# Attention on one core: the row of maxima for the queries, from four products with the identity and a copy to two transfers through memory

## The chip, the cores and the metric

The kernel runs on one core of a Trainium2 chip. Its engines are TensorE (PE in the profile, its weight loads PEld), VectorE (DVE), ScalarE (ACT), GpSimd (POOL) and SyncE (SP), which here issues transfers; 16 DMA engines move the data. Each engine works through its own list of instructions in order and waits on semaphores for the others. The metric is the device time of one execution in microseconds; lower is better.

## The reference, cut to what matters

Two layers, each `x = x + attention(norm(x)) * silu(ffn(norm(x)))`, on 2048 tokens of width 128. Attention has 16 heads of width 64:

```python
# layer 0                                             # layer 1, with rotated q, k
scores = einsum('bhsd,bhtd->bhst', q, k) * scale      scores = einsum('bhqd,bhkd->bhqk', q, k) * SCALE
                                                      kb = -p * jnp.log1p(a * dist)
attn = softmax(scores, axis=-1)                       attn = softmax(scores + kb[None], axis=-1)
out = einsum('bhst,bhtd->bhsd', attn, v)              out = einsum('bhqk,bhkd->bhqd', attn, v)
out = einsum('bsf,fm->bsm', out, WO[0])               out = out @ out_w.T
```

Scores are large, so the softmax needs each query's maximum subtracted before the exponential. In this kernel the scores stand transposed, keys on partitions and queries along the free dimension; the maxima must therefore lie in a row along the queries.

## The kernel before

`attention_stage` runs once for each layer. The work of a layer is cut into 64 chunks (`NCH`): 16 heads (`H`) by 4 groups of 512 queries (`NC`, `QC`). A chunk `n` has 8 steps (`NS`), each with 256 keys. The order of each engine is written out by hand.

What happens to the maxima, by the lines of the profile:

- TensorE, `maxima(n, j)` (L652, L653): 128 queries by 1024 keys, into the PSUM buffer `jb` (in the first two chunks also into the two halves of `st`). VectorE reduces each product to one maximum for each query (`maxima`: L845 in layer 0; in layer 1 L840, which adds the bias table on the way) and signals `max_done`; only then may TensorE write `jb` again. This runs two chunks ahead (`AHEAD`).
- VectorE, `merge(n)` (L851): eight partial maxima for each partition become `m4`, four numbers on each of 128 partitions.
- ScalarE, `divide_maxima(n)` (L772): `m4` divided by 128 is written as fp16 into `m4w`, spread over 128 columns in layer 0 and over two columns (0 and 64, of an otherwise zero tile) in layer 1.
- TensorE, `row(n)` (L663): four products of `m4w` with the identity put the numbers along the free dimension of `xb`, a PSUM buffer that the sums (`sums_of`, L710) and the projection (`project`, L719) use too.
- ScalarE, `row(n)` (L777): `xb` is copied to `rows[:, n % 2, :]`, fp16, and signals `row_done`.
- Use: `scores(n, s)` on TensorE (L688) accumulates q times k in three rounds of two products and, in a fourth, `lower` times `rows`, which subtracts the maxima. In layer 0 only every other step has the fourth round; in the others VectorE subtracts (`subtract_maxima`, L865), reading `rows` from SBUF. In layer 1 all steps have it, and VectorE adds the bias table (`add_bias`, L878). Then ScalarE takes the exponential (L784, L788, L795), GpSimd adds up the sums (L943 to L950), and TensorE multiplies by the values (`values`, L699).

The row of chunk `n + 1` is made inside chunk `n`: at step 5 in layer 0 and at step 1 in layer 1 (`ROW_STEP`); the sums of the chunk before stand at step 3, its projection at step 7 or 5. TensorE takes the steps of layer 0 in pairs: a maxima product, scores of two steps, a second maxima product, whatever `between` puts there, values of two steps. Such a pair is called a slot below. Ahead of the loop TensorE makes all maxima products of chunk 0, the row of chunk 0, and the maxima products of chunk 1.

SP's queue holds the loads of the queries and keys of a head, high and low halves (`qh`, `kh`, `ql`, `kl`, eight transfers of 256 KB), and in layer 1 the bias table (`tab`). The loads of head `h` wait until the loads of the head before have landed and the scores of head `h - 2` have been read.

Of the kernel before, what the change touches and what calls it, by code (L numbers as in the profile page):

```python
# [11 lines left out]
P = 128  # L12
D = 128
S = 2048
# [23 lines left out]
SUM_STEP, ROW_STEP, OUT_STEP = (3, 3), (5, 1), (7, 5)  # L38
# [526 lines left out]
def attention_stage(nc, k, layer, bias=False):  # L565

    with ExitStack() as ctx:
# [6 lines left out]
        m4w = m.sb(g + "m4w", [P, 4, P], F16)  # L574
# [16 lines left out]
        row_ready, row_done = m.sem(g + "row_ready"), m.sem(g + "row_done")  # L591
# [7 lines left out]
        sum_step, row_step, out_step = SUM_STEP[layer], ROW_STEP[layer], OUT_STEP[layer]  # L599
# [19 lines left out]
        def _(sp):  # L619
            for h in range(H):  # L620
                if h >= 1:
                    sp.wait_ge(loaded, 16 * loads * h)
                    sp.wait_ge(low_loaded, 16 * 4 * h)
                if h >= 2:
                    sp.wait_ge(st_read, NS * NC * (h - 1))
# [7 lines left out]
                if h == 0:  # L633
                    sp.wait_ge(loaded, 16 * loads)
                for low in (slice(0, DH), slice(DH, P)):
                    sp.dma_start(ql[low, at], k.qk_low[0, pr][half, :]).then_inc(low_loaded, 16)
                    sp.dma_start(kl[low, at], k.qk_low[1, pr][half, :]).then_inc(low_loaded, 16)

        @block.tensor
        def _(pe):  # L640
# [15 lines left out]
            def row(n):  # L656
                pe.wait_ge(m4_done, n + 1)
                if bias and n >= 3:
                    pe.wait_ge(proj_done, n - 2)
                if not bias and n >= 2:  # L660
                    pe.wait_ge(rs_done, n - 1)
                for t in range(4):
                    last = nc.tensor.matmul(xb[:, t * P:(t + 1) * P], m4w[:, t, :], k.ident16[:, :],  # L663
                                            start=True, stop=True)
                last.then_inc(row_ready, 1)

            def scores(n, s):
# [3 lines left out]
                if s == 0:  # L671
                    pe.wait_ge(row_done, n + 1)
# [31 lines left out]
            def sums_of(n):  # L704
                pe.wait_ge(folded, n + 1)
                pe.wait_ge(row_done, min(n + (3 if bias else 2), NCH))
# [7 lines left out]
            def project(n):  # L714
                pe.wait_ge(ov_saved, n + 1)
                pe.wait_ge(rs_done, n + 1)
                pe.wait_ge(row_done, min(n + 3, NCH))
# [8 lines left out]
            row(0)  # L726
# [6 lines left out]
            def between(n, s):  # L733
                if s == row_step and n + 1 < NCH:
                    row(n + 1)
# [643 lines left out]
```

## Time and profile before

| | |
|---|---|
| time, median of 3 runs | 3077.13 us (3074.41 to 3077.42) |
| the profiled execution | 3079.59 us |
| its span, first to last instruction | 3077.9 us |
| TensorE busy | 2807.8 us, 91% |
| VectorE busy | 2504.0 us, 81% |
| GpSimd busy | 2502.6 us, 81% |
| ScalarE busy | 1557.4 us, 51% |
| packets of all transfers | 63825, of these 18017 under 512 B |

Times in the rows are microseconds from the start of the span. Attention of layer 0 lies between about 194 and 1435, that of layer 1 between about 1731 and 3067; what stands before, between and behind is norms, feed-forward parts and the making of q, k and v. A row of a timeline gives start, length, engine, line, operation and operands; the bracket at its end, where there is one, is the time the engine sat idle before it and what it waited for. Products that follow one another are pipelined, so their lengths overlap.

### The profile page before, as it was taken

To read this page: it belongs to the slowest core of one execution; us is meant where nothing else is said; L and a number is where in the kernel's file an instruction comes from. 1 tells how busy PE (TensorE), PEld (TensorE's weight loads), DVE (VectorE), ACT (ScalarE), POOL (GpSimd) and SP (SyncE) were. 2 spreads that over 40 slices of the span, in tenths; PEclk is the share of its full clock that TensorE was granted. 3 is DMA by queue.
4 is the path that set the end of the run, shared out by engine and by line. 5 is a ranking of instruction groups with operands and counts; after the bars stand their busy time and mean duration, and the time that the engine had idled before them with its cause. 6 is when DMAs were issued, how large, how long until landed. Compare 5 with 4: busy or idle time off the path is not lost. (4 is left out here: it accounts for less than half of the span.)

```text
span 3077.9 us, 46733 instructions
## 1 busy us (share of the span) xinstructions
PE 2807.8 (91%) x17656; PEld 1147.6 (37%) x17656; DVE 2504.0 (81%) x3379; ACT 1557.4 (51%) x1889; POOL 2502.6 (81%) x1205
## 2 busy tenths in 40 slices
PE   5959999999999999996499599999999999999997
PEld 3413333333333333333354133333333333333332
DVE  6568888888888888874339699999999999999995
ACT  4325555555555555552122255555555555555554
POOL 0009999999999999994339389999999999999997
PEclk9979999999999999997699699999999999999998
DMA  4250111111111111101203501111111111111100
GB/s 109 86 191 22 35 29 28 28 28 28 28 28 28 28 29 28 28 1 38 60 27 137 190 4 52 55 55 55 55 55 55 55 55 55 55 55 55 55 1 14
DMA packets 63825, 155.28 MB, mean 50 GB/s; under 512 B 18017, under 2 KB 33770, under 8 KB 61426
## 3 DMA queue, kind: packets, MB, share of 16 engines
q1 hardware_dynamic: 62578, 150.20, 17.4%
q8 instruction: 141, 2.31, 0.3%
q0 software_dynamic: 1024, 2.10, 0.2%
q14 instruction: 82, 0.67, 0.1%
HBM read 113.34 MB, written 38.93 MB: 49 GB/s over the span
## 5 line engine op out<-in xcount | busy, mean ns | idle before, releaser
L943 POOL TENSOR_TENSOR a_sums<-a_sums,room 128x1024 f32<-128x1024 f32 x512 | 1195.4, 2364 | 83.1 <-ACT room L795 42.5
L699 PE MATMUL a_ov<-room,va 128*64 128x512 f32 x4096 | 994.0, 606 | 0.0
L784 ACT ACTIVATE room<-room,sscale 128x1024 f32<-128x1024 f32 x512 | 588.3, 1149 | 539.3 <-DVE room L878 539.2
L845 DVE TENSOR_REDUCE a_mx<-a_jb 128x1 f32<-128x1024 f32 x501 | 611.9, 1221 | 129.6 <-PE a_jb L653 123.4
L943 POOL TENSOR_TENSOR a_sums<-room 128x1024 f32<-128x1024 f32 x256 | 604.3, 2361 | 116.6 <-ACT room L784 66.8
L840 DVE CUSTOM_DVE_ANT_0 a_junk<-a_jb,a_tab 128x1024 bf16<-128x1024 f32 x501 | 610.5, 1219 | 83.2 <-PE a_jb L653 74.8
L878 DVE TENSOR_TENSOR room<-a_st,a_tab 128x1024 f32<-128x1024 f32 x512 | 622.9, 1217 | 12.4 <-PE a_st L688 10.2
L795 ACT ACTIVATE room<-a_st,sscale 128x1024 f32<-128x1024 f32 x256 | 285.3, 1114 | 360.1 <-PE a_st L688 360.1
L652 PE MATMUL a_jb<-a_kh,a_qh 64*128 64x512 f16 x1002 | 384.9, 384 | 66.1 <-DVE a_mx L840 32.1
L699 PEld LDWEIGHTS a_ov<-room,va 128*64 128x64 f32 x4096 | 248.7, 136 | 409.3 <-issue 372.7
L688 PE MATMUL a_st<-a_qh,a_kh 64*128 64x512 f16 x2048 | 395.6, 383 | 3.0 <-DVE a_mx L840 2.9
L688 PE MATMUL a_st<-a_ql,a_kh 64*128 64x512 f16 x2048 | 390.8, 378 | 0.0
L688 PE MATMUL a_st<-a_qh,a_kl 64*128 64x512 f16 x2048 | 390.6, 378 | 0.0
L865 DVE SCALAR_TENSOR_TENSOR room<-a_rows,a_st 128x1024 f32<-128x1024 f16 x256 | 312.7, 1221 | 92.3 <-PE a_st L688 90.9
L653 PE MATMUL a_jb<-a_kh,a_qh 64*128 64x512 f16 x1002 | 385.1, 384 | 0.0
L788 ACT ACTIVATE room<-room,sscale 128x1024 f32<-128x1024 f32 x256 | 294.0, 1148 | 170.8 <-DVE room L865 170.8
L946 POOL TENSOR_TENSOR a_sums<-a_sums 128x1024 f32<-128x1024 f32 x128 | 302.8, 2366 | 10.1
L688 PE MATMUL a_st<-a_rows,a_lower 64*128 64x512 f16 x1536 | 292.9, 378 | 0.0
L652 PEld LDWEIGHTS a_jb<-a_kh,a_qh 64*128 64x128 f16 x1002 | 93.6, 93 | 465.8 <-DVE a_mx L845 306.3
L688 PEld LDWEIGHTS a_st<-a_qh,a_kh 64*128 64x128 f16 x2048 | 99.8, 94 | 274.0 <-issue 164.1
L950 POOL TENSOR_TENSOR a_total<-a_sums 128x512 f32<-128x512 f32 x128 | 162.5, 1270 | 10.0
L710 PE MATMUL a_xb<-ones,a_total 128*128 128x1 f32 x1024 | 136.4, 254 | 17.3 <-POOL a_total L950 17.3
(219 smaller groups left out, 2642.6 us busy)
## 6 DMA issues: line engine op xcount, KB each, us to landing
a_tab<-bias_line SPq DMA_DIRECT2D x16, 1984.0 KB, 11.0
qk_high<-q_oh SPq DMA_DIRECT2D x32, 512.0 KB, 2.6
qk_low<-q_ol SPq DMA_DIRECT2D x32, 512.0 KB, 3.6
a_qh<-qk_high SPq DMA_DIRECT2D x64, 256.0 KB, 4.5
a_kh<-qk_high SPq DMA_DIRECT2D x64, 256.0 KB, 5.1
a_ql<-qk_low SPq DMA_DIRECT2D x64, 256.0 KB, 7.5
a_kl<-qk_low SPq DMA_DIRECT2D x64, 256.0 KB, 7.8
ex_w<-in_L_ffn_W SPq DMA_DIRECT2D x1, 2048.0 KB, 10.5
```

The costliest lines, as they stand in the source:

```text
L652: nc.tensor.matmul(o[:, 0:QC], qh[0:DH, q0:q0 + P], kh[0:DH, k0:k0 + QC], start=True, stop=True)
L653: nc.tensor.matmul(o[:, QC:2 * QC], qh[DH:P, q0:q0 + P], kh[DH:P, k0 + QC:k0 + 2 * QC], start=True, stop=True).then_inc(max_ready, 1)
L688: last = nc.tensor.matmul(st[:, step % 2, t * QC:(t + 1) * QC], w, x, start=(r == 0), stop=(r == len(rounds) - 1))
L699: last = nc.tensor.matmul(ov[t * DH:(t + 1) * DH, :], k.va[:, 2 * s + t, h * DH:(h + 1) * DH], prob[:, step % RING, t * QC:(t + 1) * QC], ...
L784: nc.scalar.activation(prob[:, r, :], prob[:, r, :], ACT.Exp, scale=k.sscale[:, layer:layer + 1])\
L788: nc.scalar.activation(prob[:, r, :], prob[:, r, :], ACT.Exp, scale=k.sscale[:, 0:1])\
L840: nc.vector.tensor_tensor_reduce(out=junk[:, i % 2, :], in0=scratch(n, j), in1=tab[:, n // NC % 2, c0:c0 + 2 * QC][:, ::-1], scale=1.0, sc ...
L845: nc.vector.reduce_max(mx[:, j // 2, j % 2:j % 2 + 1], scratch(n, j), AX.X).then_inc(max_done, 1)
L865: nc.vector.scalar_tensor_tensor(p, high, -float(MAXROW), x, ALU.mult, ALU.add).then_inc(lowered, 1)
L878: nc.vector.tensor_tensor(p[:, :, ::-1], x[:, :, ::-1], window, ALU.add).then_inc(added, 1)
L943: nc.gpsimd.tensor_tensor(a, first, prob[:, step % RING, :], ALU.add).then_inc(summed, 1)
L946: nc.gpsimd.tensor_tensor(a, a, sums[:, (n + 1) % 2, :], ALU.add).then_inc(summed, 1)
```

## The change

`m4` divided by 128 becomes `m4h`, 128 partitions by 4 numbers in fp16. SP stores it into a row of memory, `max_row[layer, n]`, as 512 single elements in the order of the queries, waits for the store, and loads that row into all 128 partitions of `rows[:, n % 2, :]` with one transfer. TensorE's `row(n)`, ScalarE's `row(n)`, the tile `m4w` and its memset go, and with them the waits that kept `xb` apart from the row. Those who waited for `row_done` wait for `row_in`. The loads of a head stand in SP's queue behind a row's broadcast.

```diff
-        m4w = m.sb(g + "m4w", [P, 4, P], F16)
+        m4h = m.sb(g + "m4h", [P, 4], F16)
...
+            def spread_row(n):
+                sp.wait_ge(m4_done, n + 1)
+                sp.dma_start(k.max_row[layer, n].rearrange("(t p) -> p t", p=P), m4h[:, :],
+                             allow_slow_non_contiguous=True).then_inc(row_stored, 16)
+                sp.wait_ge(row_stored, 16 * (n + 1))
+                if n >= 2:
+                    sp.wait_ge(st_ready, NS * (n - 1))
+                    if not bias:
+                        sp.wait_ge(lowered, NS // 2 * (n - 1))
+                sp.dma_start(rows[:, n % 2, :], k.max_row[layer, n:n + 1, :].broadcast_to([P, QC])).then_inc(row_in, 16)
+
+            high_and_bias(0)
+            sp.wait_ge(loaded, 16 * loads)
+            low_halves(0)
+            spread_row(0)
+            sp.wait_ge(low_loaded, 16 * 4)
+            high_and_bias(1)
+            low_halves(1)
+            for n in range(NCH - 1):
+                sp.wait_ge(row_in, 16 * (n + 1))
+                spread_row(n + 1)
+                h = n // NC + 1
+                if n % NC == 0 and 2 <= h < H:
+                    sp.wait_ge(loaded, 16 * loads * h)
+                    sp.wait_ge(low_loaded, 16 * 4 * h)
+                    sp.wait_ge(st_read, NS * NC * (h - 1))
+                    high_and_bias(h)
+                    low_halves(h)
...
-            def row(n):
-                pe.wait_ge(m4_done, n + 1)
-                if bias and n >= 3:
-                    pe.wait_ge(proj_done, n - 2)
-                if not bias and n >= 2:
-                    pe.wait_ge(rs_done, n - 1)
-                for t in range(4):
-                    last = nc.tensor.matmul(xb[:, t * P:(t + 1) * P], m4w[:, t, :], k.ident16[:, :],
-                                            start=True, stop=True)
-                last.then_inc(row_ready, 1)
-
...
                 if s == 0:
-                    pe.wait_ge(row_done, n + 1)
+                    pe.wait_ge(row_in, 16 * (n + 1))
...
                 if n >= 1:
-                    act.wait_ge(row_ready, n)
-                wide = m4w[:, :, 0:DH + 1:DH] if bias else m4w[:, :, :]
-                nc.scalar.activation(wide, m4[:, :].unsqueeze(2).broadcast_to([P, 4, 2 if bias else P]), ACT.Copy,
-                                     scale=1.0 / MAXROW).then_inc(m4_done, 1)
-
-            def row(n):
-                act.wait_ge(row_ready, n + 1)
-                nc.scalar.activation(rows[:, n % 2, :], xb[:, :], ACT.Copy).then_inc(row_done, 1)
+                    act.wait_ge(row_stored, 16 * n)
+                nc.scalar.activation(m4h[:, :], m4[:, :], ACT.Copy, scale=1.0 / MAXROW).then_inc(m4_done, 1)
```

TensorE inside the loop of layer 0, the end of the slot with the row, before:

```order
L652 MATMUL a_jb<-a_kh,a_qh 128x512 [waits a0_max_done]
L653 MATMUL a_jb<-a_kh,a_qh 128x512
L663 MATMUL a_xb<-ident,a_m4w 128x128 [waits a0_rs_done,a0_m4_done]
L663 MATMUL a_xb<-ident,a_m4w 128x128 x3
L699 MATMUL a_ov<-room,va 64x512 [waits a0_exp_done]
```

The same place in the changed kernel, where a slot with the row now reads like the empty one:

```order
L678 MATMUL a_jb<-a_kh,a_qh 128x512 [waits a0_max_done]
L679 MATMUL a_jb<-a_kh,a_qh 128x512
L714 MATMUL a_ov<-room,va 64x512 [waits a0_exp_done]
L714 MATMUL a_ov<-room,va 64x512
L714 MATMUL a_ov<-room,va 64x512 [waits a0_exp_done]
```

The row's four products, and their wait for the divided maxima, are gone between the maxima product and the values.

TensorE ahead of the loop of layer 0, from the last two maxima products of chunk 0 to the first of chunk 1, before:

```order
L652 MATMUL a_st<-a_kh,a_qh 128x512 [waits a0_max_done]
L653 MATMUL a_st<-a_kh,a_qh 128x512
L663 MATMUL a_xb<-ident,a_m4w 128x128 [waits a0_m4_done]
L663 MATMUL a_xb<-ident,a_m4w 128x128 x3
L652 MATMUL a_jb<-a_kh,a_qh 128x512 [waits a0_max_done]
L653 MATMUL a_jb<-a_kh,a_qh 128x512
```

And in the changed kernel:

```order
L678 MATMUL a_st<-a_kh,a_qh 128x512 [waits a0_max_done]
L679 MATMUL a_st<-a_kh,a_qh 128x512
L678 MATMUL a_jb<-a_kh,a_qh 128x512 [waits a0_max_done]
L679 MATMUL a_jb<-a_kh,a_qh 128x512
L678 MATMUL a_st<-a_kh,a_qh 128x512 [waits a0_max_done]
```

The wait for the divided maxima of chunk 0 no longer stands ahead of chunk 1's first maxima product.

SP in layer 0 of the changed kernel, around the loads of head 2 (`a0_m4_done` is ScalarE's signal that `m4h` is written, `a0_row_in` that a broadcast landed):

```order
L638 DMA max_row<-a_m4h 128x4x1 [waits a0_m4_done,a0_row_in]
L645 DMA a_rows<-max_row 128x512 [waits a0_lowered,a0_st_ready,a0_row_stored]
L624 DMA a_qh<-qk_high 64x2048 [waits a0_exp_done,a0_low_loaded,a0_loaded]
L625 DMA a_kh<-qk_high 64x2048
L624 DMA a_qh<-qk_high 64x2048
L625 DMA a_kh<-qk_high 64x2048
L633 DMA a_ql<-qk_low 64x2048
L634 DMA a_kl<-qk_low 64x2048
L633 DMA a_ql<-qk_low 64x2048
L634 DMA a_kl<-qk_low 64x2048
L638 DMA max_row<-a_m4h 128x4x1 [waits a0_m4_done,a0_row_in]
```

In the kernel before, that queue held the eight loads alone, head behind head; now each row's store and broadcast stand among them.

## Rows read from the trace of the kernel before

**Rows 1.** Stretches inside layers 0 and 1: us, busy by engine, clock, DMA, GB/s

```profile
630.00:930.00 300.00, 294.21 (x2004) 117.23 (x2002) 249.63 (x291) 169.91 (x179) 283.75 (x130) 1.00 0.13 29
2300.00:2600.00 300.00, 291.35 (x1961) 110.09 (x1963) 279.30 (x388) 169.74 (x225) 281.55 (x134) 1.00 0.20 56
```

The busy columns are TensorE, its weight loads, VectorE, ScalarE and GpSimd.

**Rows 2.** Timeline of TensorE in layer 0: row's slot, projection's end, empty slot

```profile
607.13 0.39 PE L652 MATMUL a_jb<-a_kh,a_qh 64*128 64x512 f16 x1
...
609.18 0.40 PE L663 MATMUL a_xb<-ident,a_m4w 128*128 128x128 f16 x4
609.51 1.94 PE L699 MATMUL a_ov<-room,va 128*64 128x512 f32 x8
611.49 0.39 PE L652 MATMUL a_jb<-a_kh,a_qh 64*128 64x512 f16 x1
...
614.63 1.94 PE L699 MATMUL a_ov<-room,va 128*64 128x512 f32 x8
616.50 0.39 PE L652 MATMUL a_jb<-a_kh,a_qh 64*128 64x512 f16 x1
...
620.85 0.39 PE L652 MATMUL a_jb<-a_kh,a_qh 64*128 64x512 f16 x1 [0.32 <-DVE a_mx L845]
```

**Rows 3.** Timeline of VectorE in the slot with the row, layer 0

```profile
609.08 1.22 DVE L865 SCALAR_TENSOR_TENSOR room<-a_rows,a_st 128x1024 f32<-128x1024 f16 x1 [0.29 <-PE a_st L688]
...
610.22 1.22 DVE L845 TENSOR_REDUCE a_mx<-a_jb 128x1 f32<-128x1024 f32 x1
```

**Rows 4.** Timeline of all engines around the row in layer 1

```profile
2213.49 0.40 PE L663 MATMUL a_xb<-ident,a_m4w 128*128 128x128 f16 x4
2213.62 1.22 DVE L840 CUSTOM_DVE_ANT_0 a_junk<-a_jb,a_tab 128x1024 bf16<-128x1024 f32 x1
...
2213.82 0.39 PE L688 MATMUL a_st<-a_qh,a_kh 64*128 64x512 f16 x2
...
2214.89 0.09 PEld L652 LDWEIGHTS a_jb<-a_kh,a_qh 64*128 64x128 f16 x1 [0.53 <-DVE a_mx L840]
```

**Rows 5.** Timeline ahead of the loops: layer 0, then layer 1

```profile
211.07 0.63 ACT L772 ACTIVATE a_m4w<-a_m 128x512 f16<-128x512 f32 x1 [23.77 <-DVE a_m L851]
...
213.01 1.22 DVE L845 TENSOR_REDUCE a_mx<-a_jb 128x1 f32<-128x1024 f32 x1 [2.04 <-PE a_jb L653]
...
222.61 0.63 PE L688 MATMUL a_st<-a_qh,a_kh 64*128 64x512 f16 x2
...
1753.08 0.24 ACT L772 ACTIVATE a_m4w<-a_m 128x8 f16<-128x8 f32 x1 [22.75 <-DVE a_m L851]
...
1754.66 1.23 DVE L840 CUSTOM_DVE_ANT_0 a_junk<-a_jb,a_tab 128x1024 bf16<-128x1024 f32 x1 [1.67 <-PE a_jb L653]
...
1764.05 0.61 PE L688 MATMUL a_st<-a_qh,a_kh 64*128 64x512 f16 x2 [2.91 <-DVE a_mx L840]
```

**Rows 6.** Timeline: maxima divided in layers 0 and 1; first scores of layer 1's next chunk

```profile
604.54 0.62 ACT L772 ACTIVATE a_m4w<-a_m 128x512 f16<-128x512 f32 x1
...
2212.99 0.23 ACT L772 ACTIVATE a_m4w<-a_m 128x8 f16<-128x8 f32 x1
...
2227.63 0.39 PE L688 MATMUL a_st<-a_qh,a_kh 64*128 64x512 f16 x2
```

**Rows 7.** Transfers alike: an issue and who waited; issues, KB, us to landing

```profile
27.16 0.43 SPq L183 DMA_DIRECT2D tf_b<-in_L_ffn_b  x1
...
30.41 1.15 ACT L211 ACTIVATE tf_mag<-tf_w 128x512 f32<-128x512 f32 x2 [4.48 <-DMA tf_b<-in_L_ffn_b]
...
bias_line<-line SPq DMA_DIRECT2D x1, 256.0 KB, 2.0
...
rt_gain<-in_L_ffn_ln_g SPq DMA_DIRECT2D x1, 64.0 KB, 2.9
```

**Rows 8.** A head's last load in layer 1: its issue, then us to landing

```profile
2253.32 0.68 SPq L637 DMA_DIRECT2D a_kl<-qk_low  x1
...
a_kl<-qk_low SPq DMA_DIRECT2D x2, 256.0 KB, 11.9
```

More of the change, by code:

```diff
@@ L37 @@
 NJ = 8
-SUM_STEP, ROW_STEP, OUT_STEP = (3, 3), (5, 1), (7, 5)
+SUM_STEP, OUT_STEP = (3, 3), (7, 5)
 class Memory:
@@ L590, in attention_stage @@
         merged, m4_done = m.sem(g + "merged"), m.sem(g + "m4_done")
[L591 removed]
+        row_stored, row_in = m.sem(g + "row_stored"), m.sem(g + "row_in")
         st_ready, exp_done = m.sem(g + "st_ready"), m.sem(g + "exp_done")
@@ L598, in attention_stage @@
                                                                                    if bias else None)
-        sum_step, row_step, out_step = SUM_STEP[layer], ROW_STEP[layer], OUT_STEP[layer]
+        sum_step, out_step = SUM_STEP[layer], OUT_STEP[layer]
         lowered = None if bias else m.sem(g + "lowered")
@@ L619, in _, with high_and_bias @@
         def _(sp):
[L620 to L625, printed above, removed]
+            def high_and_bias(h):
                 at = slice((h % 2) * S, (h % 2 + 1) * S)
@@ L632, in _, with low_halves @@
                     sp.dma_start(tab[:, h % 2, :], k.bias_rows(h)).then_inc(loaded, 16)
-                if h == 0:
-                    sp.wait_ge(loaded, 16 * loads)
+            def low_halves(h):
+                at = slice((h % 2) * S, (h % 2 + 1) * S)
+                pr, half = h // 2, slice((h % 2) * DH, (h % 2 + 1) * DH)
                 for low in (slice(0, DH), slice(DH, P)):
@@ L725, in _ @@
                 maxima(0, j)
-            row(0)
             for j in range(NJ):
@@ L733, in between @@
             def between(n, s):
-                if s == row_step and n + 1 < NCH:
-                    row(n + 1)
                 if s == sum_step and n >= 1:
@@ L814, in _ @@
             divide_maxima(0)
-            row(0)
             for n in range(NCH):
@@ L822, in _ @@
                         divide_maxima(n + 1)
-                    if s == row_step and n + 1 < NCH:
-                        row(n + 1)
                     if bias and s == out_step and n >= 1:
@@ L857, in subtract_maxima @@
                 if s == 1:
-                    ve.wait_ge(row_done, n + 1)
+                    ve.wait_ge(row_in, 16 * (n + 1))
                 if step >= RING:
@@ L919, in _ @@
         def _(pool):
-            pieces = (flat(m4w[:, :, :]), lower[:, :], flat(k.acc[:, :, :]))
+            pieces = (lower[:, :], flat(k.acc[:, :, :]))
             for piece in pieces:
@@ L1328, in build @@
         k.qk_low = nc.dram_tensor("qk_low", (2, H // 2, P, S), F16, kind="Internal").ap()
+        k.max_row = nc.dram_tensor("max_row", (2, NCH, QC), F16, kind="Internal").ap()
         k.bias_line = nc.dram_tensor("bias_line", (H, LINE), F32, kind="Internal").ap()
```

2 lines of the change are left out of this document (removed).

## The prediction

> **What bounds the kernel now.** I read the stretches of the two attention stages first. In both, TensorE is busy 97 to 98% of the time at a granted clock of 1.00, GpSimd about 94%, VectorE 83 and 93%, ScalarE 57% [rows 1]. That invites a quick answer: take matmuls away from TensorE and the time falls by their length. A busy TensorE need not be the engine that ends a slot, though, so the second view is its timeline through one chunk of layer 0.
>
> A chunk of layer 0 has four slots. Each begins with a maxima product into `jb`, runs scores and a second maxima product, and ends with the products of probabilities and values. One slot also holds the sums, one the row, one the projection, and one nothing extra. The slot with the row goes from 607.13 to 611.49, which is 4.36 us; the empty slot from 616.50 to 620.85, 4.35 us [rows 2]. The row's four products move the next TensorE work by 609.51 - 609.18 = 0.33 us, and yet the slot is no longer than the one without them. What ends both slots stands on VectorE. The empty slot's end says so itself: its last row waits for `a_mx` on VectorE [rows 2]. In the row's slot VectorE waits 0.29 us for the scores, subtracts the maxima from 609.08, and reduces the second maxima product from 610.22 for 1.22 us, until 611.44 [rows 3]. TensorE begins the next maxima product at 611.49: `jb` is one buffer, and is free only then. By its own work TensorE would have been ready 1.87 us (the length of such a block where nothing holds it, 614.63 to 616.50) after 609.51, at 611.38 [rows 2]. So the row lies in 0.33 us that TensorE would otherwise have spent waiting.
>
> In layer 1 the row stands after the maxima product of step 1. It goes from 2213.49 to 2213.82, one block of scores follows, and the weights of the next maxima product are loaded at 2214.89, after a wait of 0.53 us that the row puts down to `a_mx` on VectorE. VectorE's reduction that frees `jb` runs from 2213.62 for 1.22 us, to 2214.84 [rows 4], 0.05 us before. So here too VectorE sets the slot's end.
>
> **The change part by part.** *Products removed.* Layer by layer 64 rows of 0.33 us go, 128 x 0.33 = 42 us of TensorE's work. In the steady loop (63 rows in each layer) I count nothing for them: cover is the chain scores, subtraction, reduction in layer 0 and back-to-back VectorE work in layer 1, neither of which reads `xb`. In layer 0 the removal makes at best 4.36 into 4.35 us, 63 x 0.01 = 0.6 us. If that cover were absent, they would be worth the whole 42 us.
>
> *ScalarE.* The widened copy of 0.62 us becomes one of 128x4, about 0.23 us by the 128x8 form [rows 6], and a 128x512 copy from PSUM (about 0.6 us) goes. ScalarE is busy 57% [rows 1] and neither copy stands before an exponent that is late, so this counts zero. What it does is to set the time at which the store may go.
>
> *The first rows.* Before the loop TensorE stops at the row of chunk 0 until the maxima are divided, and only then begins the maxima products of chunk 1, so VectorE sits idle: 2.04 us in layer 0 and 1.67 us in layer 1 [rows 5]. With the row gone TensorE goes on, its three buffers are free in turn, and VectorE passes from the merge to chunk 1 at once. The stages' first scores wait for VectorE's sixteenth reduction. That takes 2.04 + 1.67 = 3.7 us off, provided the row itself is there in time.
>
> *The two transfers.* From the division of the maxima to the first scores that read the row there are these spans. In layer 0's loop from 604.54 + 0.23 = 604.8 [rows 6] to 616.50 [rows 2], 11.7 us. In layer 1's loop from 2212.99 + 0.23 = 2213.2 to 2227.63, 14.4 us [rows 6]. In the first chunk of layer 0 from 211.07 + 0.23 = 211.3 to 222.61 - 2.04 = 220.6, 9.3 us; of layer 1 from 1753.32 to 1764.05 - 1.67 = 1762.4, 9.1 us [rows 5]. The trace has no store of 2-byte pieces, so I bound it by neighbours. From below: a store of whole rows to memory lands 2.0 us after its issue [rows 7]. From above: the load of `tf_b` has the same 512 single elements, 4 bytes each; it is issued at 27.16 behind that stage's weights, and the work that waits for all of them starts at 30.41, so it had landed within 3.2 us [rows 7]. I take 3.2, the row nearest in shape. The broadcast of one row to 128 partitions is like that of `rt_gain`, 2.9 us, with other loads ahead of it [rows 7]; from below it can hardly beat the 2.0 us of the store. Together 4.0 to 6.1 us, and with 6.1 still 3.0 us before the earliest deadline. So they are hidden in all four places, and count zero. With the cover gone each microsecond over costs 63 us in layer 0.
>
> That load shows 512 separate pieces costing little. It writes SBUF, however, and the new store writes memory, where no row has pieces so small. The Trainium skill (DMA: Bandwidth & Descriptors, Specifications) says that an engine carries out transfers below 512 B as read-modify-write; no run here shows it, and the page has no price for it. By the row the term is zero; by the page it would be the slow store below.
>
> *SP's queue.* Each row adds two issues there, and waits for the divided maxima, the store and the broadcast. Behind them queue the loads of the next head, which in the loop now leave after the row's broadcast is issued instead of at the chunk's start. In layer 1 these are nine issues of some 0.6 us, and the last such transfer lands 11.9 us after its issue [rows 8], some 17 us after the first issue. Now they begin about 4 us after the division (3.2 for the store, 0.6 for an issue), land some 21 us after it, and their first reader comes two chunks (40 us) later. The next row's store comes one chunk, 20 us, after the last; at worst it queues for 1 us behind their tail, against 14.4 - 6.1 = 8.3 us to spare. In layer 0, where only half as much is loaded, they are gone by then. Cost zero.
>
> **Sum.** The profiled execution took 3079.59 us, its span is 3077.9. 3079.59 - 3.7 - 0.6 = 3075.3. That execution lies 2.5 us over the median of the runs, 3077.13, so the forecast is 3072.8 us, 0.14% less. A measurement of this kernel tells some 0.2% (6.2 us) from no change, so this counts as the same.
>
> **The rivals.** *TensorE is the bound after all*: removed work comes back in full, 3077.1 - 42 - 4 = 3031 us. For it speak 98% [rows 1]; against it the two equal slots [rows 2]. A part of it is likelier, such as 0.1 to 0.3 us in one layer, 6 to 20 us: 3053 to 3067. It would need VectorE's chain to shorten too, and nothing in the change shortens it.
>
> *A slow store, the slower side.* Each of the 16 DMA engines has 32 pieces. Should they go one at a time to memory, the deadline in layer 0 falls when the store takes over 11.7 - 2.9 = 8.8 us, that is (8.8 - 2.0) / 32 = 0.21 us a piece. At 0.25 us the store takes 10.0 us, each of 63 chunks is 1.2 us longer: 3072.8 + 76 = 3149, with another 2.9 us in each first chunk, some 3155 us. Layer 1's 14.4 us would still hold. Against it speaks the load of the same number of pieces within 3.2 us.
>
> *The prologue's gain is lost.* If store and broadcast take 11 us, some 2 us more than the first chunks give them, they still fit into 11.7 and 14.4 us in the loop, but VectorE's 2.04 and 1.67 us turn into TensorE's wait for the row: 3076.5, no change. I count this with the main case.
>
> *Loads and rows in each other's way* at the 28 head changes that the loops have: if the next row waited so long behind the loads that its span were overrun by 0.2 to 0.6 us each time, 3078 to 3090. It decides from 8.3 us behind the tail in layer 1, and by the sum above 1 us is the most.
>
> **How the numbers follow.** Hidden transfers with all or some of the first chunks' gain 0.74 (3069.5 to 3079 with the runs' spread of 3 us; 0.05 of it falls below 3071, which is faster by over 0.2%). TensorE's time back in full 0.04, in part 0.07. Slow store 0.07. Loads and rows colliding 0.05, half of it over 3083. Something unnamed that is slower 0.03. So faster 0.16, slower 0.12 (0.07 + 0.02 + 0.03), same 0.72. For the range 0.8 is wanted: the main case, the better half of the partial gain and the collisions give 0.74 + 0.03 + 0.05, so from 3062 to 3086.
>
> **What would show it.** In the trace after: no products with `m4w`; a slot of layer 0 without sums and projection still 4.35 us, VectorE's reduction ending 0.05 us before TensorE's maxima product; VectorE's idle time ahead of chunk 1 near zero in both layers; the store landing in 2 to 3.2 us and the broadcast in 2 to 2.9; no wait of TensorE for `a_rows`; 64 x 512 more packets under 512 B in each layer. A row slot shorter than 4.3 us would prove the first rival; scores that wait for the broadcast in every chunk of layer 0 the second.

## The result: 4076.85 us, a third slower

| | before | after |
|---|---|---|
| time, median | 3075.78 us (3074.41 to 3077.42, 4 runs) | 4076.85 us (4058.95 to 4079.02, 4 runs) |
| ratio to before, 95% interval | | 1.3242 (1.3203 to 1.328) |
| profiled execution; its span | 3079.59; 3077.9 us | 4076.74; 4075.0 us |
| mean clock granted to TensorE over the span (1.00 is 2.4 GHz) | 0.964 | 0.867 |

The forecast was 3072.8 us, the range 3062 to 3086. It was wrong: the kernel is 1001 us slower. Three lines of the changed kernel's page: busy time by engine, the costliest group of scores on TensorE (busy, mean ns | idle time ahead of it and what ended it), and the broadcasts.

```profile
PE 3021.1 (74%) x17144; PEld 1176.7 (29%) x17144; DVE 2508.2 (62%) x3379; ACT 1472.6 (36%) x1761; POOL 2501.2 (61%) x1203
...
L703 PE MATMUL a_st<-a_qh,a_kh 64*128 64x512 f16 x2048 | 450.8, 437 | 802.7 <-DMA a_rows<-max_row 796.6
...
a_rows<-max_row SPq DMA_DIRECT2D x128, 128.0 KB, 4.5
```

TensorE has 512 instructions fewer than before, the row's products, and yet is busy longer: 3021.1 us instead of 2807.8. It is idle for 796.6 us ahead of scores that wait for the row's broadcast. The same two stretches as in [rows 1] (us; busy by TensorE, weight loads, VectorE, ScalarE, GpSimd; clock, DMA, GB/s):

```profile
630.00:930.00 300.00, 220.86 (x1326) 82.68 (x1328) 170.59 (x198) 106.66 (x110) 196.90 (x90) 0.88 0.18 27
2600.00:2900.00 300.00, 232.68 (x1411) 84.22 (x1410) 207.91 (x287) 119.94 (x154) 208.49 (x100) 0.88 0.21 47
```

Where 2004 matmuls ran in 300 us of layer 0, 1326 do now, and the granted clock is 0.88 instead of 1.00. SP's timeline in layer 0, the issues of one store, its broadcast and the next store:

```profile
721.54 0.37 SPq L638 DMA_DIRECT2D max_row<-a_m4h  x1
734.97 0.32 SPq L645 DMA_DIRECT2D a_rows<-max_row  x1
748.52 0.37 SPq L638 DMA_DIRECT2D max_row<-a_m4h  x1
```

SP issues the broadcast as soon as the store has landed, so the store takes 13.4 us. The prediction had 3.2. The next row, 27.0 us later, shows the new period. TensorE and VectorE where that broadcast lands, with two earlier rows of TensorE that bound a slot of the same chunk which has neither sums nor projection, the row's former slot:

```profile
723.86 0.39 PE L678 MATMUL a_jb<-a_kh,a_qh 64*128 64x512 f16 x1
728.22 0.39 PE L678 MATMUL a_jb<-a_kh,a_qh 64*128 64x512 f16 x1 [0.37 <-DVE a_mx L846]
...
739.42 0.61 PE L703 MATMUL a_st<-a_qh,a_kh 64*128 64x512 f16 x2 [5.81 <-DMA a_rows<-max_row]
...
742.63 1.22 DVE L866 SCALAR_TENSOR_TENSOR room<-a_rows,a_st 128x1024 f32<-128x1024 f16 x1 [7.68 <-PE a_st L703]
```

From 734.97 to 739.42 the broadcast takes 4.4 us (2.9 predicted). TensorE has waited 5.81 us for it, and its next products take 0.61 us instead of 0.39, the 1.2 GHz level. The slot without extra work, 723.86 to 728.22, is 4.36 us long and ends in a wait for VectorE, as in [rows 2].

So each chunk is now one closed chain: maxima divided, store, broadcast, first scores, and some steps later the next chunk's maxima divided. The starts of the 128 divisions in ScalarE's timeline give the periods; the first of each layer is left out of the means. In layer 0 they go from 18.61 to 27.00 us in the mean, 63 x 8.39 = 529 us. In layer 1 they go from 20.20 to 27.54, 63 x 7.34 = 462 us. Together that is 991 of the 997 us by which the spans of the two profiled executions differ.

When do the pieces move? Two stretches behind the store at 721.54 (columns as above):

```profile
722.50:723.00 0.50, 0.50 (x6) 0.21 (x4) 0.50 (x1) 0.50 (x1) 0.00 (x0) 1.00 0.49 18
723.00:734.50 11.50, 10.24 (x68) 3.67 (x64) 9.39 (x14) 4.84 (x5) 10.50 (x5) 1.00 0.01 1
```

The DMA engines are half busy for half a microsecond, then almost idle (a share of 0.01) for 11.5 us, until the store counts as landed. The store's time is not in packets that engines handle one behind the other; it lies after them. The Trainium skill (DMA: Bandwidth & Descriptors, Anatomy of one DMA) says, of transfers that GpSimd issues, that the semaphore can only be raised once the last byte is confirmed in the target memory, and puts most of a fixed 2 us there. This transfer is SP's; its trace agrees on the place, not on the size: from 723.04, when the last 2-byte packet has moved, to 734.97 are 11.9 us.

### The profile page after: what moved, and what is told of

It is laid out like the page before. It is cut to its first block and busy times, and to the rows that moved or that the text cites. A ratio compares the mean times of both kernels' runs of the same rounds, so it can differ in the third digit from the quotient of the medians.

```text
span 4075.0 us, 45958 instructions
## 1 busy us (share of the span) xinstructions
PE 3021.1 (74%) x17144; PEld 1176.7 (29%) x17144; DVE 2508.2 (62%) x3379; ACT 1472.6 (36%) x1761; POOL 2501.2 (61%) x1203
## 5 line engine op out<-in xcount | busy, mean ns | idle before, releaser
L703 PE MATMUL a_st<-a_qh,a_kh 64*128 64x512 f16 x2048 | 450.8, 437 | 802.7 <-DMA a_rows<-max_row 796.6
L714 PE MATMUL a_ov<-room,va 128*64 128x512 f32 x4096 | 1040.4, 630 | 0.0
L879 DVE TENSOR_TENSOR room<-a_st,a_tab 128x1024 f32<-128x1024 f32 x512 | 622.9, 1217 | 30.4 <-PE a_st L703 28.2
L678 PE MATMUL a_jb<-a_kh,a_qh 64*128 64x512 f16 x1002 | 421.5, 421 | 62.1 <-DVE a_mx L846 34.0
L703 PE MATMUL a_st<-a_ql,a_kh 64*128 64x512 f16 x2048 | 450.7, 437 | 0.0
L703 PE MATMUL a_st<-a_qh,a_kl 64*128 64x512 f16 x2048 | 448.5, 434 | 0.0
L679 PE MATMUL a_jb<-a_kh,a_qh 64*128 64x512 f16 x1002 | 421.5, 421 | 0.0
L714 PEld LDWEIGHTS a_ov<-room,va 128*64 128x64 f32 x4096 | 262.0, 144 | 499.9 <-issue 419.7
L703 PE MATMUL a_st<-a_rows,a_lower 64*128 64x512 f16 x1536 | 334.7, 432 | 0.0
L703 PEld LDWEIGHTS a_st<-a_qh,a_kl 64*128 64x128 f16 x2048 | 112.8, 107 | 159.0 <-issue 66.4
## 6 DMA issues: line engine op xcount, KB each, us to landing
a_tab<-bias_line SPq DMA_DIRECT2D x16, 1984.0 KB, 14.4
```

The source lines that it names most:

```text
L678: nc.tensor.matmul(o[:, 0:QC], qh[0:DH, q0:q0 + P], kh[0:DH, k0:k0 + QC], start=True, stop=True)
L679: nc.tensor.matmul(o[:, QC:2 * QC], qh[DH:P, q0:q0 + P], kh[DH:P, k0 + QC:k0 + 2 * QC], start=True, stop=True).then_inc(max_ready, 1)
L703: last = nc.tensor.matmul(st[:, step % 2, t * QC:(t + 1) * QC], w, x, start=(r == 0), stop=(r == len(rounds) - 1))
L714: last = nc.tensor.matmul(ov[t * DH:(t + 1) * DH, :], k.va[:, 2 * s + t, h * DH:(h + 1) * DH], prob[:, step % RING, t * QC:(t + 1) * QC], ...
L879: nc.vector.tensor_tensor(p[:, :, ::-1], x[:, :, ::-1], window, ALU.add).then_inc(added, 1)
```

## Experiments: what the store waits for

**Trial transfers.** The kernel before, with single transfers from SP put behind the head loads of layer 0, each waited for; the code is cut to two of ten kinds:

```diff
+            def store_2(i):        # 512 x 2 B, adjacent
+                sp.dma_start(k.t_2[i].rearrange("(t p) -> p t", p=P), k.ident16[:, 0:4], ...).then_inc(probed, 16)
+            def store_2_at_64(i):  # 512 x 2 B, 64 B apart
+                sp.dma_start(k.t_2_64[i, :, 0].rearrange("(t p) -> p t", p=P), k.ident16[:, 0:4], ...).then_inc(probed, 16)
...
+                        probes[i % len(probes)](i // len(probes))
+                        sp.wait_ge(probed, 16 * (i + 1))
```

> The kernel before, with its row as it was, and beside it trial transfers on SP's otherwise idle queue in layer 0, four of each kind, one at a time, each waited for; nothing else waits for them, so the time stays near 3077. What is read is the time from a trial's issue to the next issue. Kinds: store of 512 pieces of 2 bytes next to one another (the change's own), load of the same, broadcast of a 1 KB row, store of 512 pieces of 4 bytes side by side, of 2 bytes each 64 bytes apart, of 2 bytes each 512 bytes apart, of 128 pieces of 8 bytes side by side, of 128 pieces of 2 bytes side by side, of 512 pieces of 64 bytes, of 512 pieces of 512 bytes. Theory A, each small write to memory costs its DMA engine a fixed time, (13.4 - 2.0) / 32 = 0.36 us: all kinds of 512 pieces under 512 bytes take 13 us, both kinds of 128 pieces 2.0 + 8 x 0.36 = 4.9 us. Theory B, writes into the same few bytes of memory stand in line: 13 us side by side, about 3 us at 64 or 512 bytes apart, 128 pieces some 5 us, 64-byte pieces 3 us. Theory C, 512 pieces are slow to issue or to count whichever way they go: the load takes 13 us too. By A and B the load stays under 3.2 us.

SP's timeline; from one issue to the next is the length of the first transfer, where a trial follows a trial (the last of a group of three is followed by the next head's loads and can't be read). `t` is the trial row of memory, L623 the adjacent 512 x 2 B, L641 the load of that row as 512 pieces, L629 and L632 512 x 2 B at 64 and at 512 B, L638 128 adjacent x 2 B, L626 512 adjacent x 4 B, L635 128 adjacent x 8 B:

```profile
217.94 0.38 SPq L623 DMA_DIRECT2D t<-ident  x1
232.03 0.38 SPq L641 DMA_DIRECT2D a_rows_back<-t  x1
235.56 0.33 SPq L650 DMA_DIRECT2D a_rows_back<-t  x1
...
386.55 0.34 SPq L638 DMA_DIRECT2D t<-ident  x1
402.29 0.37 SPq L644 DMA_DIRECT2D t<-gate  x1
...
539.01 0.37 SPq L626 DMA_DIRECT2D t<-gate  x1
548.08 0.36 SPq L629 DMA_DIRECT2D t<-ident  x1
...
612.35 0.34 SPq L635 DMA_DIRECT2D t<-ident  x1
615.03 0.33 SPq L638 DMA_DIRECT2D t<-ident  x1
...
834.30 0.36 SPq L629 DMA_DIRECT2D t<-ident  x1
836.07 0.37 SPq L632 DMA_DIRECT2D t<-ident  x1
838.03 0.33 SPq L635 DMA_DIRECT2D t<-ident  x1
```

| transfer | us, issue to next issue |
|---|---|
| store, 512 x 2 B adjacent | 12.9 to 14.1 |
| the same 512 pieces loaded into SBUF | 2.6 to 4.0 |
| that 1 KB row broadcast to 128 partitions | 2.9 |
| store, 512 x 2 B, 64 B apart; 512 B apart | 1.8 to 3.0; 1.8 to 2.0 |
| store, 512 x 4 B adjacent | 8.1 to 10.5 |
| store, 128 x 8 B adjacent | 2.7 to 3.9 |
| store, 128 x 2 B adjacent | 15.7 to 16.3 |
| store, 512 x 64 B; 512 x 512 B | 1.8 to 2.0; 2.3 |

Theory B holds in kind; it is not the count of pieces, and not their size: 512 pieces of 2 B are quick once they lie 64 B apart. The price is for small writes close together in memory; the load of the same pieces, which writes SBUF, is quick, which is why it was a bad neighbour to judge by. The surprise is that a quarter as many adjacent pieces take longer, 16 us against 13.

**How close together.** Other stores in the same place, all of 2-byte pieces from one column of a tile: 8, 32 and 64 adjacent ones, and 128 with gaps.

```diff
+            probes = (few(8), few(32), few(64), apart(2), apart(4), apart(8), apart(16))
```

> The kernel before with trial stores from SP in layer 0, each waited for, of 2-byte pieces out of one column of a tile. The changed kernel's store took 13.4 us; the first trial transfers gave some 13.3 us for 512 adjacent pieces of 2 bytes, 16 us for 128 adjacent ones, 2.2 us for 512 pieces that lie 64 B apart. Theory L (pieces that fall into the same 64 B of memory are written one behind the other, at 13.3 / 32 = some 0.4 us each, and different 64 B go side by side): 32 adjacent pieces (one such line) cost as much as 512, some 13 us, 64 adjacent ones too; 8 adjacent pieces some 3.3 us; 128 pieces 4 B apart (16 to a line) some 7 us, 8 B apart (8 to a line) some 3.5 us, 16 B apart (4 to a line) and 32 B apart (2 to a line) some 2 us. Theory T (the time goes with the number of adjacent pieces in the whole store, whatever line they are in): 8 pieces 2 us, 32 pieces some 4 us, 64 pieces some 8 us, half of 128's. Theory G (what counts is a gap, not the line: pieces with a gap between them are quick): all four with gaps 2 us.

SP's timeline, 8 adjacent pieces, then 32, and elsewhere 64 (`t_few`), each up to the next issue:

```profile
219.95 0.29 SPq L623 DMA_DIRECT2D t_few<-ident  x1
221.12 0.32 SPq L623 DMA_DIRECT2D t_few<-ident  x1
225.21 0.48 SPq L623 DMA_DIRECT2D t_few<-ident  x1
...
460.15 0.46 SPq L623 DMA_DIRECT2D t_few<-ident  x1
469.83 0.34 SPq L629 DMA_DIRECT2D t_apart<-ident  x1
```

8 pieces 1.2 us, 32 pieces 3.1 to 4.1, 64 pieces 9.7 to 11.9; 128 pieces 4 B apart 7.4 to 8.3, 8 B apart 3.0 to 5.1, 16 B apart 1.4 to 2.3, 32 B apart 1.4 to 1.5. The two longest stores of 64, 11.6 and 11.9 us, came right behind a trial store into the same row; the two of 9.7 us did not. Theory L, lines of 64 B, falls with the 32 pieces (13 us expected). Theory T, their mere number, falls with 512 pieces being no slower than 128. Theory G falls with the gaps of 2 B. Yet nearly all of it fits a coarser line: 0.1 to 0.16 us for each piece in the same 256 B (up to 0.19 in the two stores of 11.6 and 11.9 us), with different 256 B side by side. That rule was made from these numbers, so it needed a test of its own.

**Shifting the pieces.** The same stores, begun at other places of a 1 KB row:

```diff
+            probes = (at(0, 128), at(64, 128), at(0, 64), at(32, 64), at(96, 64), two_of_128, at(0, 32))
```

> The kernel before with trial stores of adjacent 2-byte pieces from SP in layer 0, shifted against the start of a 1 KB row of memory. All trial stores so far fit one rule: some 0.12 us for each piece that falls into the same 256 B, and different 256 B side by side (32 adjacent pieces 3.1 to 4.1 us, 64 9.7, 128 16, 512 13; 128 pieces 4 B apart 7.5, 8 B apart 3 to 5, 16 B apart 2.1, 32 B apart 1.4). Theory 256 (blocks of 256 B counted from the row's start): 128 pieces from byte 0 16 us, from byte 128 (64 in each of two blocks) some 9 us; 64 pieces from byte 0 and from byte 64 9.7 us, from byte 192 (32 and 32) some 4 us; 256 pieces in two blocks some 16 us; 32 from byte 0 some 3.5 us. Theory T (the number of adjacent pieces counts, wherever they begin): the shift changes nothing, and 256 pieces take longer than 128. Theory 512 (blocks of 512 B): no change with these shifts, and 256 pieces some 30 us.

SP's timeline: 128 pieces from byte 0, then 128 from byte 128; and from another head 64 pieces from byte 64, then 64 from byte 192:

```profile
218.73 0.33 SPq L623 DMA_DIRECT2D t_line<-ident  x1
234.29 0.33 SPq L623 DMA_DIRECT2D t_line<-ident  x1
244.53 0.47 SPq L623 DMA_DIRECT2D t_line<-ident  x1
...
836.92 0.46 SPq L623 DMA_DIRECT2D t_line<-ident  x1
843.42 0.46 SPq L623 DMA_DIRECT2D t_line<-ident  x1
847.51 0.38 SPq L628 DMA_DIRECT2D t_line<-ident  x1
```

| pieces, first byte | most in one 256 B | expected by it | measured, us |
|---|---|---|---|
| 128 from 0 | 128 | 16 | 15.6 to 16.8 |
| 128 from 128 | 64 | 9 | 8.5 to 10.2 |
| 64 from 0 | 64 | 9.7 | 8.7 to 9.7 |
| 64 from 64 | 64 | 9.7 | 6.5 to 8.1 |
| 64 from 192 | 32 | 4 | 3.3 to 4.3 |
| 256 from 0 | 128 | 16 | 15.0 to 16.8 |
| 32 from 0 | 32 | 3.5 | 3.0 to 4.4 |

Moving the same 128 pieces by 128 B makes their store a third to a half shorter, and a second block of 128 adds nothing. So it is the 256 B that count, by their place in the row, and not the number of pieces. Writes into one 256 B stretch of memory stand in line; the row of 64 from byte 64 is a little quicker than the rule has it. The kernel's 512 adjacent pieces are four such stretches of 128; they took 13 us where the rule says 16, and the trials don't show why. Of what in the memory or on the way to it makes them wait these runs say nothing.

## Experiments: what the change is worth with a quick store, and what its parts are worth

**The quick store.** The changed kernel, storing each partition's four maxima as one piece of 8 B (32 pieces in 256 B). The row then has another order, so the maxima of other queries are subtracted; the work is the same.

```diff
-                sp.dma_start(k.max_row[layer, n].rearrange("(t p) -> p t", p=P), m4h[:, :],
-                             allow_slow_non_contiguous=True).then_inc(row_stored, 16)
+                sp.dma_start(k.max_row[layer, n].rearrange("(p t) -> p t", p=P), m4h[:, :]).then_inc(row_stored, 16)
```

> The changed kernel with one line different: the store writes each partition's four numbers side by side, 128 pieces of 8 bytes in place of 512 of 2. The numbers of the row then stand in another order than the queries, so the softmax subtracts the maxima of other queries; everything else is as in the changed kernel. If the 2-byte pieces are the cause of the slow store, the store lands in 2 to 5 us, store and broadcast fit into the 9 to 14 us that the row has, and the time is what the prediction gave for hidden transfers, 3070 to 3077 us. If the way through memory is slow as such (two dependent transfers, the wait on SP, the broadcast), it stays over 3500 us.

3073.26 us (3071.53 to 3075.14), ratio 0.9993 (0.9984 to 1.0002). SP's timeline in layer 0, a store and its broadcast:

```profile
731.32 0.32 SPq L638 DMA_DIRECT2D max_row<-a_m4h  x1
733.96 0.32 SPq L644 DMA_DIRECT2D a_rows<-max_row  x1
```

And the broadcasts in the page's list of transfers, the last number being the median from issue to landing:

```profile
a_rows<-max_row SPq DMA_DIRECT2D x128, 128.0 KB, 4.1
```

With a store of 2.6 us here (2.9 in the median) the periods are 18.59 and 20.21 us, those of the kernel before, and the time is 0.5 us from the forecast. That near a hit has luck in it: the forecast took off 4.3 us, and against the kernel before, 3075.69 us in the same round, 2.4 came off (4.9 less to 0.6 more by the interval). All other terms of the sum held together; how the store lays its pieces makes the difference between 3073 and 4077 by itself.

**The order kept.** The same store, with each query getting its own maximum: in layer 0 a maxima product takes every fourth query, in layer 1 TensorE reads the row with a step of 8 B.

```diff
+        def in_order(n):
+            return rows[:, n % 2, :].rearrange("k (p t) -> k t p", t=4) if bias else rows[:, n % 2, :]
...
+                at = slice(q0 + j // 2 * P, q0 + (j // 2 + 1) * P) if bias else slice(q0 + j // 2, q0 + QC, 4)
-                nc.tensor.matmul(o[:, 0:QC], qh[0:DH, q0:q0 + P], kh[0:DH, k0:k0 + QC], start=True, stop=True)
+                nc.tensor.matmul(o[:, 0:QC], qh[0:DH, at], kh[0:DH, k0:k0 + QC], start=True, stop=True)
...
-                        x = rows[half, n % 2, :] if r == 3 else queries[half, q0:q0 + QC]
+                        x = in_order(n)[half] if r == 3 else queries[half, q0:q0 + QC]
```

> The changed kernel with the store as 128 pieces of 8 bytes, and everything else put so that each query still gets its own maximum: in layer 0 a maxima product takes every fourth query, so that a partition holds four neighbouring queries; in layer 1 TensorE reads the row in memory order with a step of 8 bytes. My theory (only the store's term was wrong, a store of 8-byte pieces takes 3 us and is hidden): 3073 us like the run in which the row's order was left wrong (3073.26), a ratio of 0.999 to the kernel before. Rival (reading or loading fp16 with a step of 8 bytes costs TensorE time): 8 weight loads of a chunk in layer 0 and 8 products of 64 x 512 in layer 1 (of 64) slower; if a product with such a step takes twice its time, 8 x 0.2 us in a chunk of layer 1, up to 100 us over: 3170 us.

3161.03 us, ratio 1.0279 (1.0265 to 1.0293): the rival holds. TensorE's timeline in layer 1, at a granted clock of 1.00 (window 2300 to 2600):

```profile
2300.68 0.38 PE L706 MATMUL a_st<-a_qh,a_kl 64*128 64x512 f16 x2
2300.90 0.61 PE L706 MATMUL a_st<-a_rows,a_lower 64*128 64x512 f16 x2
2301.33 0.40 PE L681 MATMUL a_jb<-a_kh,a_qh 64*128 64x512 f16 x1
```

The pair that reads the row with a step holds TensorE from 2300.90 to 2301.33, 0.43 us, where its neighbour takes 0.22. Eight such pairs are 1.7 us more a chunk; layer 1's period went from 20.20 to 21.54, layer 0's (18.67, with stepped weight loads) hardly moved. 63 x 1.34 = 84 us is the loss, but for 2 us. So the change can be made harmless in layer 0, but this way of putting the order right in layer 1 costs more than the row's products ever did.

**The row's products taken away.** The kernel before, making the row for chunks 0 and 1 alone; from chunk 2 on old rows are subtracted.

```diff
-                if s == row_step and n + 1 < NCH:
+                if s == row_step and n + 1 < 2:
                     row(n + 1)
```

> The kernel before without the row's four products and without the copy of the row in the loop, from chunk 2 on: scores read the rows of chunks 0 and 1 again and again, so other maxima are subtracted. If VectorE ends the slots with the row, as the prediction has it, the time falls by 0 to 1 us (3075 us). If TensorE is the bound, 124 x 0.33 = 41 us come off (3035 us).

3076.03 us, ratio 1.0003 (0.9994 to 1.0013). TensorE's busy time in the page fell from 2807.8 to 2765.0 us, and nothing came of it: the 42 us lay in TensorE's waits for VectorE, as the prediction said, and the rival in which TensorE is the bound is dead, its part of 6 to 20 us too: the interval leaves 2 us at most.

**The first row moved.** The kernel before, its first row made behind the third maxima product of chunk 1:

```diff
-            row(0)
             for j in range(NJ):
                 maxima(1, j)
+                if j == 2:
+                    row(0)
```

> The kernel before with one step moved: ahead of the loop the row of chunk 0 stands behind the third maxima product of chunk 1 and not ahead of the first. If VectorE's idle time there (2.04 and 1.67 us) sits on the path, the time falls by 3.7 us, to a ratio of 0.9988; if the first chunk is held by something else, it stays at 1.000.

3072.45 us, ratio 0.9986 (0.9977 to 0.9995), the one version whose interval lies wholly below the kernel before. VectorE's timeline ahead of layer 0's loop, where [rows 5] has 2.04 us of idle time:

```profile
207.93 0.16 DVE L852 TENSOR_REDUCE a_m<-a_mx 128x4 f32<-128x8 f32 x1
208.12 1.22 DVE L846 TENSOR_REDUCE a_mx<-a_jb 128x1 f32<-128x1024 f32 x1
```

The idle time is gone. The prediction's 3.7 us (0.12%) for the two stages lie inside the interval, which reaches from 0.05 to 0.23%.

## Experiments: from a late row to 1000 us

**Delay by other means.** The quick store made three and five times over, one waiting for the other:

```diff
+                for i in range(3):
+                    if i >= 1:
+                        sp.wait_ge(row_stored, 16 * (3 * n + i))
+                    sp.dma_start(k.max_row[layer, n].rearrange("(p t) -> p t", p=P), m4h[:, :]).then_inc(row_stored, 16)
```

> The changed kernel with the quick store of 128 pieces of 8 bytes (other queries' maxima are subtracted, as in the run with the quick store), made three times over, one waiting for the other, ahead of the broadcast: 3 x 2.9 + 4.1 = 12.8 us from the divided maxima to the row. The prediction's deadlines are 11.7 us in a chunk of layer 0, 14.4 in layer 1, 9.3 and 9.1 in the first chunks. If they hold and each microsecond over is one of time: layer 0 some 1.1 us over in 63 chunks, 69 us, and 3.5 us in each first chunk: 3073 + 76 = 3150 us, layer 1 unchanged. If the clock falls as soon as TensorE waits, more: 3200 us or over. If the deadlines are too tight (others wait with the row and have room), 3080 us or under.

> The same with five quick stores, one behind the other: 5 x 2.9 + 4.1 = 18.6 us from the divided maxima to the row, near the 13.4 to 14.2 + 4.4 us of the changed kernel. Theory D (the time of the changed kernel is delay of the row and nothing else; whatever makes it, the same delay costs the same): near 4080 us, 3950 to 4200. Theory S (the slow store does more harm than its delay, as by holding the DMA engines or memory for others): well under that; by the deadlines alone (6.9 us over in layer 0, 4.2 in layer 1, 63 chunks each) 3073 + 435 + 265 + 19 = 3790 us.

3571.98 us (ratio 1.1616, 1.1595 to 1.1638) and 4640.8 us (1.5092, 1.5065 to 1.512). All the numbers expected were too small, for one reason ahead of the others: repeated like this, a store takes 3.5 to 3.9 us, not 2.9, and the broadcast 4.3. So the delays were not the ones aimed at, and the runs are to be read by the delays they had. Layer 0, medians of the delay, means of the period:

| kernel | division's end to row in | over the 11.7 us | period | longer than 18.61 by |
|---|---|---|---|---|
| quick store | 2.9 + 4.1 = 7.0 | none | 18.59 | 0 |
| three stores | 10.8 + 4.3 = 15.1 | 3.4 | 23.16 | 4.6 |
| the changed kernel | 13.75 + 4.5 = 18.25 | 6.55 | 27.00 | 8.4 |
| five stores | 18.45 + 4.3 = 22.75 | 11.05 | 31.5 | 12.9 |

The changed kernel lies between the two others, as its delay does: its time is the row's delay, whichever transfers make it. Behind the row's landing it and the kernel with five stores do alike, 8.4 and 8.2 us in the median until the next division begins. The deadline of 11.7 us from [rows 2, 6] fits too. But every row over it costs 1.2 to 1.9 us more than the overrun. Layer 1, which was expected to stay unchanged with three stores, did not: outside the chunks behind a head's loads its mean period is 21.4 us with three stores, 25.6 in the changed kernel and 30.4 with five, against 20.2, for mean delays of 15.5, 18.6 and 23.1 us and a deadline of 14.4.

**The clock.** The changed kernel with products on TensorE while it waits; the scores then overwrite them:

```diff
+                if s == 0:
+                    for i in range(12 if bias else 20):
+                        for t in range(2):
+                            half = slice(t * DH, (t + 1) * DH)
+                            nc.tensor.matmul(st[:, step % 2, t * QC:(t + 1) * QC], kh[half, base + t * P:base + (t + 1) * P],
+                                             qh[half, q0:q0 + QC], start=True, stop=True)
+                    pe.wait_ge(row_in, 16 * (n + 1))
```

> The changed kernel with work on TensorE while it waits for the row: 20 pairs of 64 x 512 products in layer 0 and 12 in layer 1, just ahead of each chunk's first scores, into the scores' buffer, which the real products then overwrite. In the changed kernel each chunk's first products behind the wait run at the 1.2 GHz level (0.61 us instead of 0.39), and from the row's landing to the next division pass 8.6 us in layer 0 and 7.8 in layer 1, against 6.9 and 5.8 us by the kernel before (its period less the prediction's deadline). Theory H (that difference is the clock): the clock stays up, the period of layer 0 falls from 27.0 by up to 1.7 us and that of layer 1 from 26.2 by up to 2.0 us, 63 chunks each: down to some 3840 us, the granted clock near 0.97. Theory N (the difference is the order of the work behind the wait, not the clock): 4077 us, or some us more where the filling runs into the row.

3966.02 us, ratio 1.2901 (1.2837 to 1.2966), 111 us less than the changed kernel. TensorE's timeline, the filling and the first scores behind the wait:

```profile
737.03 4.48 PE L698 MATMUL a_st<-a_qh,a_kh 64*128 64x512 f16 x40
742.85 0.39 PE L708 MATMUL a_st<-a_qh,a_kh 64*128 64x512 f16 x2 [1.33 <-DMA a_rows<-max_row]
```

And the two stretches:

```profile
630.00:930.00 300.00, 262.43 (x1830) 103.18 (x1832) 174.95 (x206) 108.49 (x112) 201.74 (x92) 0.97 0.16 27
2600.00:2900.00 300.00, 250.65 (x1672) 93.26 (x1672) 207.40 (x286) 120.30 (x154) 205.83 (x98) 0.93 0.19 35
```

The scores behind the wait take 0.39 us again, the clock is 0.97 in layer 0's stretch, and the median period there falls from 27.04 to 24.73 us, that of layer 1 from 26.18 to 24.41. From the row's landing to the next division pass 24.73 - 13.6 - 4.4 = 6.7 us (the division's own 0.2 among them), near the 6.9 us of the kernel before (18.61 - 11.7). So in the median chunk the part beyond the overrun goes with the 1.2 GHz level after the wait.

The whole is less than the 237 us expected, since the means, 25.69 and 26.90, stay above the medians: some chunks take 26 to 32 us in layer 0. In nearly all of them the row came later still, by a broadcast of over 5 us (mostly beside a head's loads) or a store 3 to 5 us longer, and TensorE stood idle behind the filling. Two neighbouring chunks of this run, each from the row's landing to the next division; TensorE had been idle for 7.0 us ahead of the first and for 1.8 us ahead of the second:

```profile
1421.75:1430.55 8.80, 8.77 (x45) 2.88 (x45) 3.94 (x4) 3.87 (x4) 2.35 (x1) 0.67 0.00 0
1448.98:1455.47 6.49, 6.08 (x45) 2.25 (x45) 3.96 (x4) 3.77 (x5) 2.25 (x1) 1.00 0.01 3
```

The 45 products of such a stretch take 8.8 us at a granted clock of 0.67 and 6.5 at 1.00, with next to no transfers in either (a DMA share of 0.00 and 0.01). It is so throughout layer 0 (61 chunks, without the first and the last two): in the 17 in which the clock fell to the lower level the stretch is 7.7 to 8.9 us long, in the 44 others 6.5. With three stores it is 7.7 to 9.0 in 41 chunks and 6.5 in 20; in the changed kernel the clock falls in all 61, and it is 7.8 to 8.9. So the clock, and not the order of the work, makes the part beyond the overrun.

**Loads in the way.** No run was made for this, the trace of the changed kernel shows it. SP's timeline in layer 1, the last of a head's nine loads, the next store and its broadcast:

```profile
2549.59 0.60 SPq L634 DMA_DIRECT2D a_kl<-qk_low  x1
2557.36 0.38 SPq L638 DMA_DIRECT2D max_row<-a_m4h  x1
2579.67 0.33 SPq L645 DMA_DIRECT2D a_rows<-max_row  x1
```

That store takes 22.3 us. Its pieces go behind the loads:

```profile
2557.40:2562.00 4.60, 4.30 (x30) 1.28 (x28) 4.60 (x7) 2.30 (x2) 2.38 (x1) 1.00 0.98 213
```

For 4.6 us after the store's issue the DMA engines are 0.98 busy, at 213 GB/s; the first of its 2-byte packets moves at 2563.0, 5.7 us after the issue, the last at 2565.5, and 14.1 us later it has landed. In layer 1's 15 chunks that follow a head's loads the period is 33.5 us in the mean, in the other 48 it is 25.6. So of layer 1's 462 us, 48 x 5.4 = 259 fall to ordinary chunks and 15 x 13.3 = 200 to these.

## Why the prediction was wrong, point by point

- **The store's term** is the step that failed. "I take 3.2, the row nearest in shape" took a load of 512 pieces as an upper bound for a store of 512. It was no bound: the time passes behind the DMA engines, where many small writes go into the same 256 B of memory, and no row of the trace had such writes. Measured 13.4 us against 3.2 (13.7 in the median of layer 0), and 2.9 us for the same bytes in pieces of 8. So the row that was to be hidden came some 6.5 us past its deadline chunk after chunk in layer 0, and TensorE waited for it.
- **The read-modify-write below 512 B** of the Trainium skill (DMA: Bandwidth & Descriptors, Specifications) spoke for a dear store and was put aside for want of a row. It pointed to the right side, but not by its size rule: 2-byte pieces 64 or 512 B apart land in 1.8 to 3.0 us, about as soon as 512-byte pieces (2.3 us). What the trace couldn't answer deserved more than the 0.07 that the rival got, and the upper end of the range should have followed it.
- **The slow-store rival** had the right sign and the right way to count (deadline, 63 chunks), and the wrong cause, 32 pieces one behind the other on each DMA engine. It stopped at 10.0 us, 3155, for want of a price; and it said that layer 1 would hold. A slip of 1.6 us beside it: by its own deadlines of 9.3 and 9.1 us, 10.0 + 2.9 overruns the first chunks by 3.6 and 3.8 us, not 2.9.
- **The broadcast** was taken at 2.9 us and took 4.1 to 4.5 in the median of the loop. Among the trial transfers it did take 2.9, so what lengthens it there stays open. With a quick store that is harmless; here 1.6 us of each overrun are its.
- **The cost of an overrun**, "each microsecond over costs 63 us in layer 0", is too low: 6.55 us over made 8.4, 28% more, since TensorE works at the lower clock after each wait.
- **SP's queue and the loads**, at zero, holds with the quick store (20.21 us in layer 1) and not with the slow one, where the 15 chunks behind a head's loads lose 200 us: the prediction let a store queue for 1 us behind them, and it queued for 5.7.
- **Right:** the products' worth of nothing (0.03% with them gone), the slots at 4.36 us, the first rows' 3.7 us and VectorE's gap, gone in the changed kernel too though what follows hides it; the deadline of 11.7 us; and the sum's other terms together, 3072.8 against 3073.26 with the quick store, part of it luck, as said above.

VectorE and SP ahead of layer 0's loop in the changed kernel, against [rows 5]: VectorE passes from the merge to chunk 1 at once, and later waits 11.45 us for scores that wait for the first row's store (210.63 to 223.70).

```profile
210.14 0.16 DVE L852 TENSOR_REDUCE a_m<-a_mx 128x4 f32<-128x8 f32 x1
210.34 1.23 DVE L846 TENSOR_REDUCE a_mx<-a_jb 128x1 f32<-128x1024 f32 x1
...
210.63 0.38 SPq L638 DMA_DIRECT2D max_row<-a_m4h  x1
...
223.70 0.33 SPq L645 DMA_DIRECT2D a_rows<-max_row  x1
...
232.93 1.22 DVE L866 SCALAR_TENSOR_TENSOR room<-a_rows,a_st 128x1024 f32<-128x1024 f16 x1 [11.45 <-PE a_st L703]
```

## What to carry to other kernels

A load is no measure for a store: ask where the bytes arrive, and when no row of the trace has a write of that shape, take no upper bound for the cost from the trace and time one such transfer by itself. Lay small stores so that a partition's elements go out as one piece and few pieces share 256 B, and see first what the reader then pays for the other order. A transfer in a chain that closes once per chunk cost nothing here up to its deadline, and beyond it more than its overrun where TensorE's clock fell by the wait.

## What the hardware showed

- Small writes into the same 256 B of memory (counted from the row's start) stand in line, at 0.09 to 0.19 us each (128 pieces: 15.6 to 16.8 us; 64: 6.5 to 11.9; 32: 3.0 to 4.4), different stretches side by side; in the changed kernel's store the DMA engines' share of busy time was 0.01 during that time.
- A store's packets can be through the DMA engines within 0.5 us, and the store land 12 us later.
- In layer 0 the same work behind a wait takes 6.5 us at a granted clock of 1.00, and 7.7 to 9.0 us where the clock fell to 1.2 GHz in the wait or just behind it.
- A pair of 64 x 512 products whose fp16 row is read with a step of 8 B holds TensorE for 0.43 us instead of 0.22, at the same granted clock.
